# Cross-attention and spectral FFN on one core: the context's normalising moved ahead of the zero test, its low half ahead of the slot's other additions

## The chip, the cores and the metric

One NeuronCore of a Trainium2 chip runs the whole kernel. The metric is the device time of one execution in microseconds (us); the median of three runs stands for a kernel. The engines are TensorE (PE), VectorE (DVE), ScalarE (ACT), GpSimd (POOL) and SyncE (SP); each works through its own queue in program order, and they wait for one another by semaphores.

## What is computed

Two batches of 2048 rows of width 512 pass through a cross-attention of 16 heads over 128 keys, and then through a layer that multiplies in the frequency domain. Cut to what matters:

```python
def reference(x, ctx, mask, wq, bq, wk, bk, wv, bv, wo, bo, w_freq_real, w_freq_imag, bias):
    q = layernorm(x) @ wq + bq
    k, v = ctx @ wk + bk, ctx @ wv + bv
    score = q @ k.T / sqrt(32) * mask             # per head
    score = where(score == 0, -1e9, score)
    context = softmax(score) @ v                  # per head
    x = x + context @ wo + bo
    y = real(ifft(fft(layernorm(x)) @ (w_freq_real + 1j * w_freq_imag)))
    return x + y + bias
```

The output has the shape of x, (2, 2048, 512), in float32.

## The kernel before

The 4096 rows are cut into 16 chunks (c) of 256 rows (CH). The 16 heads are four groups (g) of four heads. A step s = 4c + g is the attention of one group of heads in one chunk; there are 64 (NS). Slots v run from 2 to 79, and in each slot every engine does its part of several steps at different ages, so that the steps overlap. The order inside a slot is written out by hand in each engine's block, and so is each wait. With r the remainder of v by 4, the parts of slot v around the change are:

- **TensorE** (items of `plan`, line 37, run at lines 609 to 619): it transposes the exponentials of step v-2 (`turn`, L582, two halves), runs the fill "WO" (output projection, r = 0 or 1) or "FF" (the frequency layer as one combined matrix, r = 2 or 3), both twelve products at L438, then the scores of step v+1 (`scores`, L570), then `weigh` of step v-3, which transposes the spread reciprocals (L595) and multiplies the exponentials by the values (L599), and at last the fill "Q", a later chunk's queries (L525, twelve products). Matrices go through TensorE as a high half and a low half in float16: each pair takes three products, high by high, high by low, low by high. Up to slot 11 the middle fills are instead "V", "U" and "M", which make the values and the combined matrix.
- **ScalarE** (L747 on): it copies the transposed reciprocals of step v-4 out of PSUM (`copy_rec`, L701), makes the exponentials of step v-1 (`exps`, L688; each with a read of the accumulator) in two halves with the copy of the transposed exponentials (`copy_pt`, L697) between them, then rounds the normalised context of step v-4 to float16 (`ctx_hi`, L708), then the high halves of the fills (`hi`, L662 for queries, L667 for the combined matrix) and of x1, the rows behind the attention (`norm_hi2`, L680).
- **VectorE** (L985 on): `mask_mul` (L860) multiplies the scores of step v by the mask out of PSUM; `zero_to_neg` (L867) turns zeros into the value that the softmax drops; `ctx_norm` (L883) multiplies the context of step v-4, in PSUM, by the copied reciprocals, into the tile cn; `least` (L872) takes the minimum of each head. Then the low halves and residuals of the fills (`lo`: L833 for queries, L839 for WO, L845 for FF; `low_m`, L851), statistics of rows (L897, L940) and the reciprocals of the sums (`recip`, L877).
- **GpSimd** (L1173 on): in some slots first the powers for a standard deviation (`rstd2`, L1060 and L1063, r = 1 or 2; `stat_cols`, L1030 to L1040, r = 0). From slot 9 on it waits for the slot's zero test (L1187), then adds the output bias to x in some slots (`add_bo`, L1053). `bias` (L1093) turns the minimum of step v into the bias of the exponentials. Then come the low half of x1 (`norm_lo2`, L1068, r = 2 or 3) or the addition of the layer's bias (`add_bf`, L1079, r = 0 or 1), then `ctx_lo` (L1104), the low half of the context of step v-4 into the tile cl, then the rest of the bias additions, `spread` (L1099), which copies the reciprocals of step v-2 for TensorE, and in r = 0 the scaling of a mask (L1086).
- **SyncE** loads and stores, and turns x1's halves with transposing DMAs (`turn_x1n`, L356) that wait for both halves.

Who waits for the two moved steps: `weigh` of step s waits for the context product of step s-1 (L590), since both use the bank CX; `ctx_hi` waits for it (L705) and `ctx_lo` for `ctx_hi` (L1103). The fill WO of a chunk waits for the chunk's four low halves (L535). `ctx_norm` of step s waits for `copy_rec` of step s (L880) and for `ctx_lo` of step s-2 (L882), because cn has two buffers.

```python
            def weigh(s):
...
                if s >= 1:
                    pe.wait_ge(cn_done, s)
...
                elif kind == "WO":
                    pe.wait_ge(o_lo, 2)
                    pe.wait_ge(ch_done, 4 * c + 4)
                    pe.wait_ge(p_cl, 4 * c + 4)
```

Of the kernel before, what the change touches and what calls it, by code (L numbers as in the profile page):

```python
# [18 lines left out]
NS = 4 * NC  # L19
# [70 lines left out]
def stats_slot(c, t):  # L90
    return 3 + t if c == 4 else 4 * (c - 4) + 2 + t


def small_slot(c):
    return 2 if c == 3 else 4 * (c - 3)
# [6 lines left out]
def lo_slot(c):  # L102
    return 3 if c == 3 else 6


def bo_slot(c):

    return c + 7 if c < 3 else 4 * c + 3 if c < 13 else 2 * c + 27


def build(nc, x, xt, ctx_in, mask, wq, bq, wk, bk, wv, bv, wo, bo, lparts, tables, bf, eye, sums, pick, places, heads, out):
# [3 lines left out]
    with ExitStack() as stack:  # L115
# [666 lines left out]
        def _(dve):  # L782
# [66 lines left out]
            def low_m(c):  # L849
                dve.wait_ge(m_hi, c + 1)  # L850
                dve.scalar_tensor_tensor(out=ml[:, c, :], in0=mf[:], scalar=SO / D, in1=mh[:, c, :],  # L851
                                         op0=ALU.mult, op1=ALU.subtract).then_inc(m_lo, 1)

            def mask_mul(s):
                c = s // 4
                dve.wait_ge(sc_done, 2 * s + 2)
                dve.wait_ge(p_ms, c + 1)
                if s >= NZ:
                    dve.wait_ge(pt_done, 2 * (s - NZ) + 2)
                dve.tensor_tensor(zs[:, s % NZ], A[:].rearrange("p t (h k) -> p t h k", h=4),  # L860
                                  ms[:, c % NM].unsqueeze(2).broadcast_to([128, 2, 4, KEYS]),
                                  ALU.mult).then_inc(tt_done, 1)

            def zero_to_neg(s):
                z = zs[:, s % NZ].rearrange("p t h k -> p (t h k)")
                dve.wait_ge(tt_done, s + 1)
                dve.scalar_tensor_tensor(out=z, in0=z, scalar=0.0, in1=z, op0=ALU.is_equal,  # L867
                                         op1=ALU.subtract).then_inc(eq_done, 1)

            def least(s):  # L870
                dve.wait_ge(eq_done, s + 1)
                dve.tensor_reduce(nmin[:, s % 4, :], zs[:, s % NZ].rearrange("p t h k -> p (t h) k"),  # L872
                                  AX.X, ALU.min).then_inc(mn_done, 1)

            def recip(s):
                dve.wait_ge(ex_done, s + 1)
                dve.reciprocal(rz[:, s % 4, :], zsum[:, s % 4, :]).then_inc(rz_done, 1)  # L877

            def ctx_norm(s):
                dve.wait_ge(rc_done, s + 1)  # L880
                if s >= 2:
                    dve.wait_ge(p_cl, s - 1)  # L882
                dve.tensor_tensor(cn[:, s % 2, :], CX[:, 0:256], rec[:, s % 2, :], ALU.mult).then_inc(cn_done, 1)  # L883
# [20 lines left out]
            def fold(n):  # L904

                q, i = divmod(n, 3)
                o1, o2 = ((ALU.add, ALU.add), (ALU.subtract, ALU.add),
                          (ALU.add, ALU.subtract), (ALU.subtract, ALU.subtract))[q]
                a, b, o = ((0, 1, o1), (2, 3, o1), (0, 2, o2))[i]
                if i == 0:  # L910
                    dve.wait_ge(d_lp[q], 16)
                if i == 2:
                    dve.wait_ge(l_hi, n - 6)
                a, b = 4 * q + a, 4 * q + b
                dve.tensor_tensor(lp[:, a, :], lp[:, a, :], lp[:, b, :], o).then_inc(l_hi, 1)

            def last_lo2(t):
                n = tile_of(NC - 1, t)
                dve.wait_ge(h2_done, n + 1)
                dve.tensor_tensor(x1nl[:, t], x1[:, n % NO, :], x1nh[:, t], ALU.subtract).then_inc(l2_done, 1)  # L920
# [64 lines left out]
            for v in range(V0, V1):  # L985
                c, r = divmod(v, 4)
                held, mids = slots[v][1:]
                if 0 <= v < NS:
                    mask_mul(v)
                if 0 <= v < NS:  # L990
                    zero_to_neg(v)
                if 0 <= v - 4 < NS:
                    ctx_norm(v - 4)
                if 0 <= v < NS:
                    least(v)
                if 0 <= v - 9 < 4:
                    low_m(v - 9)
                for n in held + mids:
                    lo(n)
                tasks = []  # L1000
                tasks += [(stats1, mean1, a, t) for a in range(4, NC) for t in range(2) if stats_slot(a, t) == v]
                if r == 0 and 0 <= c - 2 < NC:
                    tasks.append((stats2, mean2, c - 2, 0))
                if r == 1 and 0 <= c - 2 < NC:
                    tasks.append((stats2, mean2, c - 2, 1))
                for stats, _, *ct in tasks:
                    stats(*ct)
                if 0 <= v - 2 < NS:
                    recip(v - 2)
                for _, mean, *ct in tasks:  # L1010
                    mean(*ct)
                if c - 2 == NC - 1 and r < 2:
                    last_lo2(r)
                if v in (4, 5):
                    for n in range(3 * v - 6, 3 * v - 3):
                        fold(n)

        @block.gpsimd
        def _(pool):
# [69 lines left out]
            def bias(s):  # L1089
                pool.wait_ge(mn_done, s + 1)  # L1090
                if s >= 4:
                    pool.wait_ge(ex_done, s - 3)
                pool.tensor_scalar(nbias[:, s % 4, :], nmin[:, s % 4, :], NEG, None, ALU.mult).then_inc(p_nb, 1)  # L1093
# [7 lines left out]
            def ctx_lo(s):  # L1101
                c, g = divmod(s, 4)
                pool.wait_ge(ch_done, s + 1)  # L1103
                pool.tensor_tensor(cl[:, c % 2, g, :], cn[:, s % 2, :], ch[:, c % 2, g, :],  # L1104
                                   ALU.subtract).then_inc(p_cl, 1)
# [19 lines left out]
            def constant_row():  # L1125

                pool.wait_ge(g_done, at["U", 3] + 1)
                pool.memset(tb[0:1, 0, :], 0.5).then_inc(dc_done, 1)
# [44 lines left out]
            for v in range(V0, V1):  # L1173
                c, r = divmod(v, 4)
                if v == 8:
                    constant_row()
                if v <= VP and 0 <= v - 3 < NS:
                    spread(v - 3)
                for a in range(5, NC):
                    if small_slot(a) == v:  # L1180
                        stat_cols(a)
                if r == 1 and 0 <= c - 2 < NC:
                    rstd2(c - 2, 0)
                if r == 2 and 0 <= c - 2 < NC:
                    rstd2(c - 2, 1)
                if VS <= v < NS:
                    pool.wait_ge(eq_done, v + 1)  # L1187
                for a in range(5, NC):
                    if v == 4 * a - 11:
                        split_lo(a, slice(0, 2), False)  # L1190
                    if v == 4 * a - 10:
                        split_lo(a, slice(2, 4))
                for a in range(3, NC):
                    if bo_slot(a) == v:
                        add_bo(a, 0)
                    if bo_slot(a) + 1 == v and a >= 12:
                        add_bo(a, 1)
                if 0 <= v < NS:
                    bias(v)
                if r == 2 and 0 <= c - 2 < NC - 1:  # L1200
                    norm_lo2(c - 2, 0)
                if r == 3 and 0 <= c - 2 < NC - 1:
                    norm_lo2(c - 2, 1)
                if r < 2 and 0 <= c - 3 < NC:
                    add_bf(c - 3, r)
                if v == 3:
                    low_o()
                if 0 <= v - 4 < NS:
                    ctx_lo(v - 4)
                for a in (3, 4):  # L1210
                    if small_slot(a) == v:
                        stat_cols(a)
                for a in range(3):
                    if bo_slot(a) == v:
                        add_bo(a, 0)
                        add_bo(a, 1)
                for a in range(3, 12):
                    if bo_slot(a) == v:
                        add_bo(a, 1, slice(0, D // 2), False)
                    if bo_slot(a) + 3 == v:  # L1220
                        add_bo(a, 1, slice(D // 2, D))
                for a in (3, 4):
                    if lo_slot(a) == v:
                        split_lo(a)
                if v >= VP and 0 <= v - 2 < NS:
                    spread(v - 2)
                if r == 0 and 2 <= c + 1 < NC:
                    scale_mask(c + 1)
# [98 lines left out]
```

## Time and profile before

| | us |
|---|---|
| runs before | 460.48, 460.57, 462.78 |
| median | 460.57 |
| the profiled execution | 462.53 |
| its span | 460.7 |
| granted clock, mean over the span | 0.996 of full speed |

| engine | busy in the span, us |
|---|---|
| TensorE, matmuls | 443.5 |
| VectorE | 399.7 |
| ScalarE | 373.1 |
| GpSimd | 362.7 |

The profile is of one execution. The span runs from the first to the last instruction; the time has some 1.8 us more around it. Busy time is the sum of what an engine executed; waiting for a semaphore isn't counted. In a time line a row gives start and duration, the engine, the line, the operation, output and inputs, how many instructions were merged, and in brackets the idle time ahead of it with the engine and line that ended it. In a list of waits a row gives who waited for whom, the sum in us, how many times, and the longest.

### The profile page before, as it was taken

What the parts mean: (1) busy time and instruction counts of PE and PEld (TensorE: products, weight loads), DVE (VectorE), ACT (ScalarE), POOL (GpSimd) and SP (SyncE); (2) the same over time, 40 slices, a digit from 0 to 9 for tenths busy, and PEclk for the clock granted to TensorE, in tenths of its full rate; (3) what the DMA queues carried; (4) which work ended last, traced back from release to release, by engine and by line L of the source; (5) the groups of instructions that cost most, each with busy time, mean ns of one, the idle gap of its engine ahead of it and who ended that gap; (6) DMA issues with size and microseconds to landing.
All of it is one profiled execution on the core that took longest, in us unless ns stands there. A gap on an engine that the chain in (4) does not pass through costs nothing.

```text
span 460.7 us, 11172 instructions
## 1 busy us (share of the span) xinstructions
PE 443.5 (96%) x3510; PEld 293.2 (64%) x3510; DVE 399.7 (87%) x630; ACT 373.1 (81%) x1434; POOL 362.7 (79%) x540
## 2 busy tenths in 40 slices
PE   7989898998999999999999999999999999999997
PEld 5777676675666666666666666666666666555444
DVE  3797599899999999999999999999999898999443
ACT  3358587889898989899989898999989888999620
POOL 6588754795889899797989897979899686976663
PEclk9999999998999999999999999999999999999999
DMA  8997653322435454545545545355433334331244
GB/s 286 393 366 183 231 190 72 106 74 72 95 83 140 125 142 117 140 121 133 125 133 110 144 108 149 84 144 125 120 90 73 92 74 98 70 93 23 70 106 123
DMA packets 85287, 60.16 MB, mean 131 GB/s; under 512 B 40141, under 2 KB 72813, under 8 KB 84718
## 3 DMA queue, kind: packets, MB, share of 16 engines
q1 hardware_dynamic: 84508, 59.29, 47.4%
q8 instruction: 29, 0.48, 0.4%
q14 instruction: 28, 0.23, 0.2%
q10 hardware_dynamic: 722, 0.17, 0.2%
HBM read 29.33 MB, written 8.39 MB: 82 GB/s over the span
## 4 chain that ended last, share of the span: by engine, by line
PE 77%; DVE 10%; issue 4%; DMA 3%; SPq 2%; ACT 2%; POOL 1%; DVEq 0%; POOLq 0%; ACTq 0%
PE bank L438 33%; PE bank L525 17%; PE bank L582 10%; PE bank L599 7%; PE scores L570 5%; DVE zs L860 3%; PE bank L595 3%; PE bank L443 2%; SPq L276 2%; DMA cxs<-in_ctx 2%; DMA xs<-in_x 1%; DVE zs L867 1%; DVE nmin L872 1%; DVE st L897 1%; PE scores L443 1%
## 5 line engine op out<-in xcount | busy, mean ns | idle before, releaser
L688 ACT ACTIVATE zs<-zs,nbias 128x128 f32<-128x128 f32 x512 | 199.6, 397 | 5.2 <-POOL nbias L1093 5.2
L688 ACT ACTIVATION_READ_ACCUMULATOR zs<-zs,nbias 128x1 f32 x512 | 99.5, 194 | 0.0
L867 DVE SCALAR_TENSOR_TENSOR zs<-zs 128x1024 f32<-128x1024 f32 x64 | 80.7, 1262 | 2.3
L860 DVE TENSOR_TENSOR zs<-scores,ms 128x1024 f32<-128x1024 f32 x64 | 78.0, 1218 | 0.3 <-issue 0.3
L872 DVE TENSOR_REDUCE nmin<-zs 128x8 f32<-128x1024 f32 x64 | 77.4, 1209 | 0.1
L525 PE MATMUL bank<-xth,wqh 128*128 128x256 f16 x256 | 70.9, 277 | 2.9 <-DVE kl L810 2.0
L697 ACT COPY pt<-bank 128x512 f32<-128x512 f32 x128 | 68.5, 587 | 5.7 <-PE bank L582 5.2
L525 PE MATMUL bank<-xth,wql 128*128 128x256 f16 x256 | 70.2, 274 | 0.0
L525 PE MATMUL bank<-xtl,wqh 128*128 128x256 f16 x256 | 70.2, 274 | 0.0
L582 PE MATMUL bank<-ident,zs 128*128 128x128 f32 x512 | 67.0, 274 | 0.5 <-ACT zs L688 0.4
L1053 POOL TENSOR_TENSOR xs<-xs,bob 128x512 f32<-128x512 f32 (+1 forms) x41 | 42.3, 1035 | 24.6 <-DVE zs L867 24.6
L582 PEld LDWEIGHTS bank<-ident,zs 128*128 128x128 f32 x512 | 56.9, 141 | 5.2 <-ACT zs L688 3.5
L438 PE MATMUL bank<-woh,ch 128*128 128x512 f16 x128 | 48.5, 379 | 1.4 <-POOL cl L1104 1.4
L701 ACT COPY rec<-bank 128x256 f32<-128x256 f32 x64 | 23.9, 373 | 31.6 <-PE bank L599 31.4
L438 PE MATMUL bank<-woh,cl 128*128 128x512 f16 x128 | 48.5, 379 | 0.0
L438 PE MATMUL bank<-wol,ch 128*128 128x512 f16 x128 | 48.5, 379 | 0.0
L1104 POOL TENSOR_TENSOR cl<-cn,ch 128x256 f16<-128x256 f32 x64 | 44.9, 701 | 1.6 <-ACT ch L708 1.6
L438 PE MATMUL bank<-mh,x1h 128*128 128x512 f16 x120 | 45.5, 379 | 0.0
L438 PE MATMUL bank<-ml,x1h 128*128 128x512 f16 x120 | 45.5, 379 | 0.0
L438 PE MATMUL bank<-mh,x1l 128*128 128x512 f16 x120 | 45.5, 379 | 0.0
L833 DVE TENSOR_TENSOR ql<-bank,qh 128x256 f16<-128x256 f32 x64 | 26.7, 422 | 21.4 <-ACT qh L662 20.6
L525 PEld LDWEIGHTS bank<-xth,wqh 128*128 128x128 f16 x256 | 25.1, 98 | 27.7 <-issue 16.5
(118 smaller groups left out, 965.3 us busy)
## 6 DMA issues: line engine op xcount, KB each, us to landing
xs<-in_x SPq DMA_DIRECT2D x16, 512.0 KB, 4.1
xtr<-in_xt SPq DMA_DIRECT2D x16, 512.0 KB, 4.5
out<-x SPq DMA_DIRECT2D x31, 256.0 KB, 2.5
qs<-qh SPq DMA_DIRECT2D x120, 64.0 KB
lp<-in_lparts SPq DMA_DIRECT2D x4, 1024.0 KB, 9.7
qs<-ql SPq DMA_DIRECT2D x60, 64.0 KB
ms<-in_mask SPq DMA_DIRECT2D x16, 128.0 KB, 2.3
wqs<-in_wq SPq DMA_DIRECT2D x2, 512.0 KB, 6.5
```

The lines of the kernel that those rows point to most:

```text
L438: last = pe.matmul(o, a, b, start=(i == 0), stop=(i == len(mm) - 1))
L525: last = pe.matmul(o[:, 0:256], a, b, start=(i == 0), stop=(c > 1 and i == 11))
L582: last = pe.transpose(PB[f][:, a:a + 128], zs[:, s % NZ, t, 2 * f + i, :], ident[:])
L599: last = pe.matmul(CX[32 * j:32 * j + 32, 0:256], vs[:, b, h:h + 32], pt[:, s % 2, j, :], start=True, stop=True)
L688: last = act.activation(z, z, ACT.Exp, bias=nbias[:, s % 4, i:i + 1], scale=-NEG, accum_out=zsum[:, s % 4, i:i + 1])
L697: act.copy(pt[:, s % 2, 2 * f:2 * f + 2, :], PB[f][:]).then_inc(pt_copied, 1)
L833: last = dve.tensor_tensor(ql[:, c % 2, f, :], src[:, 0:256], qh[:, c % 2, f, :], ALU.subtract)
L860: dve.tensor_tensor(zs[:, s % NZ], A[:].rearrange("p t (h k) -> p t h k", h=4), ms[:, c % NM].unsqueeze(2).broadcast_to([128, 2, 4, KEYS]) ...
L867: dve.scalar_tensor_tensor(out=z, in0=z, scalar=0.0, in1=z, op0=ALU.is_equal, op1=ALU.subtract).then_inc(eq_done, 1)
L872: dve.tensor_reduce(nmin[:, s % 4, :], zs[:, s % NZ].rearrange("p t h k -> p (t h) k"), AX.X, ALU.min).then_inc(mn_done, 1)
L1053: i = pool.tensor_tensor(z, z, bob[:, n], ALU.add)
L1104: pool.tensor_tensor(cl[:, c % 2, g, :], cn[:, s % 2, :], ch[:, c % 2, g, :], ALU.subtract).then_inc(p_cl, 1)
```

## The change

On VectorE `ctx_norm` of slot v goes from behind `zero_to_neg` to ahead of it. On GpSimd `ctx_lo` goes from behind `norm_lo2`, `add_bf` and `low_o` to the place right behind `bias`. No operation is added or taken out, and no wait is changed.

```diff
@@ VectorE, loop over the slots
                 held, mids = slots[v][1:]
                 if 0 <= v < NS:
                     mask_mul(v)
+                if 0 <= v - 4 < NS:
+                    ctx_norm(v - 4)
                 if 0 <= v < NS:
                     zero_to_neg(v)
-                if 0 <= v - 4 < NS:
-                    ctx_norm(v - 4)
                 if 0 <= v < NS:
                     least(v)
@@ GpSimd, loop over the slots
                 if 0 <= v < NS:
                     bias(v)
+                if 0 <= v - 4 < NS:
+                    ctx_lo(v - 4)
                 if r == 2 and 0 <= c - 2 < NC - 1:
                     norm_lo2(c - 2, 0)
...
                     add_bf(c - 3, r)
                 if v == 3:
                     low_o()
-                if 0 <= v - 4 < NS:
-                    ctx_lo(v - 4)
```

## Rows read from the trace of the kernel before

**Rows 1.** The page: the span, and busy time (share) and instructions by engine.
```profile
span 460.7 us, 11172 instructions
PE 443.5 (96%) x3510; PEld 293.2 (64%) x3510; DVE 399.7 (87%) x630; ACT 373.1 (81%) x1434; POOL 362.7 (79%) x540
```

**Rows 2.** The chain that ended last, in time: start, us, what (225 to 245 us).
```profile
231.74 1.42 PE bank L525 x12
...
237.86 1.42 PE bank L525 x12
```

**Rows 3.** The list of waits, whole span: total us, times, longest.
```profile
ACT ch L708 <- DVE cn L883: 4.5, 6, 0.9
PE bank L438 <- POOL cl L1104: 1.4, 2, 0.8
PE bank L595 <- DVE cn L883: 1.2, 2, 0.9
```

**Rows 4.** The list of waits, 130 to 385 us.
```profile
ACT rec L701 <- PE bank L599: 23.8, 40, 1.1
DVE ql L833 <- ACT qh L662: 15.0, 31, 1.1
```

**Rows 5.** The time line of VectorE in a middle slot (start, us).
```profile
239.92 1.23 DVE L867 SCALAR_TENSOR_TENSOR zs<-zs 128x1024 f32<-128x1024 f32 x1
241.06 0.42 DVE L883 TENSOR_TENSOR cn<-bank,rec 128x256 f32<-128x256 f32 x1
```

**Rows 6.** The time line of GpSimd in the same slot.
```profile
240.13 1.60 POOL L1033 TENSOR_TENSOR rs<-ve,half 128x2 f32<-128x2 f32 x1
```

**Rows 7.** The time line of ScalarE in the same slot.
```profile
237.93 0.37 ACT L701 COPY rec<-bank 128x256 f32<-128x256 f32 x1 [1.13 <-PE bank L599]
```

**Rows 8.** The time line of TensorE in the head, its idle times from 108 us on.
```profile
110.21 0.62 PE L570 MATMUL scores<-ks,qs 102*128 102x128 f16 x8 [0.64 <-DVE zs L860]
111.85 0.50 PE L595 MATMUL bank<-ident,rzb 128*128 128x128 f32 x2 [1.02 <-issue]
...
126.08 0.41 PE L595 MATMUL bank<-ident,rzb 128*128 128x128 f32 x2 [0.23 <-issue]
```

**Rows 9.** Busy time by stretch: length, PE, PEld, DVE, ACT, POOL, granted clock, DMA.
```profile
112.00:115.70 3.70, 3.70 (x23) 1.99 (x23) 3.70 (x9) 3.17 (x13) 2.67 (x5) 0.54 0.18 55
```

**Rows 10.** The time line of VectorE in the head, 105 to 124 us.
```profile
105.48 1.71 DVE L851 SCALAR_TENSOR_TENSOR ml<-mf,mh 128x512 f16<-128x512 f32 x1 [0.56 <-ACT mh L667]
...
108.93 1.23 DVE L860 TENSOR_TENSOR zs<-scores,ms 128x1024 f32<-128x1024 f32 x1
...
111.33 0.42 DVE L883 TENSOR_TENSOR cn<-bank,rec 128x256 f32<-128x256 f32 x1
...
112.79 0.68 DVE L851 SCALAR_TENSOR_TENSOR ml<-mf,mh 128x512 f16<-128x512 f32 x1
...
119.75 1.60 DVE L851 SCALAR_TENSOR_TENSOR ml<-mf,mh 128x512 f16<-128x512 f32 x1 [0.60 <-ACT mh L667]
...
123.16 1.23 DVE L860 TENSOR_TENSOR zs<-scores,ms 128x1024 f32<-128x1024 f32 x1
```

**Rows 11.** The time line of GpSimd in the head.
```profile
105.48 1.16 POOL L1068 TENSOR_TENSOR x1nl<-x,x1nh 128x512 f16<-128x512 f32 x1
```

**Rows 12.** The time line of TensorE in the tail, the two waits for cl.
```profile
407.64 0.38 PE L438 MATMUL bank<-woh,ch 128*128 128x512 f16 x1 [0.62 <-POOL cl L1104]
...
428.32 0.38 PE L438 MATMUL bank<-woh,ch 128*128 128x512 f16 x1 [0.79 <-POOL cl L1104]
```

**Rows 13.** The time line of GpSimd in the tail.
```profile
397.90 1.40 POOL L1099 COPY rzb<-rz 128x256 f32<-128x256 f32 x1
...
426.19 0.23 POOL L1093 TENSOR_SCALAR nbias<-nmin 128x8 f32<-128x8 f32 x1 [1.36 <-issue]
...
427.51 0.67 POOL L1104 TENSOR_TENSOR cl<-cn,ch 128x256 f16<-128x256 f32 x1
```

**Rows 14.** The time line of ScalarE in the tail.
```profile
426.26 0.41 ACT L708 CAST ch<-cn 128x256 f16<-128x256 f32 x1
```

## The prediction, made before the changed kernel ran

> **What bounds the kernel now.** I read the page first: TensorE is busy 443.5 of a 460.7 us span, so only 17 us of it are idle [rows 1]. Then the chain of waits, in order of time. Between 112 and 385 us it is TensorE's own work without a break: the group of twelve query products starts at 231.74 and again at 237.86, one slot of 6.12 us [rows 2], and nearly the same spacing repeats over 40 times. In that stretch VectorE sat idle for ScalarE 15.0 us before the query residual and ScalarE 23.8 us for TensorE [rows 4]; both have slack, 0.3 to 1.1 us in most slots. What the change touches can therefore only pay where TensorE waits. The list of waits names those places: TensorE waited 1.2 us for the normalised context (cn) and 1.4 us for its low half (cl), ScalarE 4.5 us for cn [rows 3]. The time lines put them in the head, before 127 us, and in the tail, up to 428 us [rows 8, 12].
>
> **The change, part 1: the context product moves ahead of the zero test.** Nothing is added or removed: 64 products of 0.42 us and 64 zero tests of 1.23 us change places [rows 5]. The product starts 1.14 us after the operation ahead of it (241.06 against 239.92) and occupies 0.34 to 0.42 us. So cn is ready 1.14 us earlier, the zero test ends about 0.34 us later, and the minimum behind both starts when it did, give or take 0.1. No DMA is moved, and SyncE has no new step ahead of it. What is queued behind the zero test: GpSimd's gate (from slot 9 on it waits for the test before it adds the output bias) opens 0.34 us later. That is hidden: the next result, the bias for the exponentials, waits for the minimum anyway, and ScalarE has the 0.3 to 1.1 us above.
>
> In the middle stretch I cost all this at nothing: TensorE's own queue covers it, and if that cover went, each slot would pay up to 0.34 us.
>
> **In the head** it is worth more. TensorE waited 0.64 us for the masked scores of slot 11 and 1.02 us at 111.85 [rows 8]. The view calls the second "issue", but VectorE's product ran 111.33 to 111.75 [rows 10], 0.10 us before TensorE went on, so I take it for cn. Moved, the product starts at 108.93 + 1.14 = 110.07 and ends at 110.49, before the score matmuls are through (111.85 - 1.02 = 110.83). This wait goes: 1.0 us.
>
> Behind these two waits the granted clock averaged 0.54 over 3.70 us, that is mostly the lower level, 1.2 GHz [rows 9]. At full clock the same work takes 3.70 x 0.54 = 2.0 us, so the dip costs 1.7. Without the second wait TensorE idles 0.64 us there, or less, and I expect no dip. Lower bound of this term 0, upper 1.7. The Trainium skill, "TensorE: Matmul & The Clock Gate", section on the HAM clock gate, says the same in other words (idle TensorE is gated to half its rate); by it alone the dip could fall elsewhere, and the term would be 0.
>
> Part 2 has a share here: at 105.48 VectorE's residual of the combined matrix took 1.71 us, against 0.68 at 112.79 [rows 10], while GpSimd ran the low half of x1 (1.16 us) from 105.48 on [rows 11]. With the context's low half (about 0.68) first, the collision is some 0.5 us shorter. I take 0.5, bounds 0 and 1.0.
>
> These sum to 3.2 us, but VectorE is next late. At 119.75 it waited 0.60 us for ScalarE [rows 10], whose chain hangs on TensorE and moves up with it. So its masking product of slot 13 (123.16, 1.23 long) comes 0.5 + 0.6 = 1.1 us sooner and ends at 123.29; the scores follow 0.05 later and last 0.45; the context step at 126.08 [rows 8] then starts at 123.8, 2.3 us sooner. The smaller bound holds: 2.3. For new collisions with GpSimd I take 0.2 off: **head 2.1 us**, bounds 0.8 and 3.0. If the clock dips all the same, TensorE brings 1.0 + 0.5 and the 0.23 us wait at 126.08: 1.7.
>
> **Part 2: GpSimd makes cl ahead of the other additions.** 64 operations of about 0.67 us go ahead of one addition of about 1.2 us [rows 11], where the slot has one. In the middle they are needed a slot later: nothing. The transposes on SyncE's queue that take x1's low half start 0.67 us later; they are used four slots on, nothing.
>
> **In the tail** TensorE waits 0.62 and 0.79 us for cl, at 407.64 and 428.32 [rows 12], both times the output projection's first matmul. The second: GpSimd finished the bias at 426.19 + 0.23 = 426.42, then did x1's low half, and cl ran 427.51 to 428.18 [rows 13]. Its input was ready at 426.26 + 0.41 = 426.67 [rows 14]. First in the queue, cl would end at 426.67 + 0.67 = 427.34, sooner than TensorE is free (428.32 - 0.79 = 427.53): 0.8 us. The first wait gives at most 0.62, and part of it moves ScalarE's chain up, so the two add: up to 1.4.
>
> Against that: in the tail VectorE's and GpSimd's queues have almost no idle time, and they collide. At 397.90 a copy to spread the reciprocals (0.40 without hindrance) took 1.40 us because a zero test was running [rows 13]. With cl first, GpSimd must wait for ScalarE's half where it now works, some 0.4 us at the first slot of the tail, and the later zero test meets other operations. I take 0.5 off: **tail 0.9 us**, bounds -0.4 and 1.4. Waits at the other additions of the tail are covered by TensorE's groups of twelve products between them.
>
> **Sum.** 2.1 + 0.9 = 3.0 us. The profiled execution took 462.53 us (span 460.7 and 1.8 around it) and would take 459.5; it lies 1.96 above the median of 460.57, which becomes **457.6 us**. The runs may differ by just that clock dip; then the head gives 1.7 in them rather than 2.1, which is inside the range.
>
> **The rivals.** About 0.5% (2.3 us) is what a measurement of this kernel can tell from no change.
>
> 1. *Half of it.* One of the two places pays, or the clock dips again while VectorE's queue holds TensorE: 1.7 in the head and nothing in the tail gives 458.9, with a little lost 459.5. For: everything in the tail hangs on which of two engines starts first. Against: both waits are in the view with their releasers. Chance 0.27.
>
> 2. *Hidden anyway.* TensorE arrives earlier and waits for the masked scores instead, or the minimum decides all: 460.4. For: VectorE's queue is nearly full in the head, and its sum of work doesn't change. Against: the waits at 111.85 and 126.08 are for cn itself, ahead of the minimum. Chance 0.08.
>
> 3. *Slower: the zero test waits for GpSimd.* Now it starts 0.03 us behind the mask, often before GpSimd's next large operation: at 239.92 it ran 1.23 us, and GpSimd's power at 240.13 took 1.60 [rows 5, 6], some 0.9 more than it needs. Moved to 240.26 it would find that operation running and wait for it, 0.6 us. The Trainium skill, "SBUF — State Buffer", section "SBUF: two separate sides", has this as a rule: a VectorE operation with two SBUF inputs and a GpSimd one exclude each other, and whoever starts first holds the port throughout. The trace agrees so far (1.60 and 1.40 us for short operations). By it the power would no longer be held up and VectorE would. It decides once VectorE loses more than its slack, 15.0 us over 42 slots or 1.4 us in four [rows 4]. With one such collision in each of four slots, 2.4 us, 1.0 us of it comes through, in 11 groups of four 11 us; with one more in some, 2 to 5 us net of the gain: about 463. Against: only two slots of four have GpSimd's power there. Chance 0.10.
>
> 4. *The product waits itself.* If the reciprocal's copy were late, VectorE would stall ahead of the zero test. ScalarE made it at 237.93 to 238.30 [rows 7], the early product would start at 239.80: 1.5 us to spare. Were it late in the head, 0.5 us would be lost: 460. Chance 0.02.
>
> **How the numbers follow.** Forecast 0.53, with its own range of 456.3 to 458.4; rivals 0.27, 0.08, 0.10, 0.02. The range takes in the bounds of head and tail together (0.8 - 0.4 = 0.4 us at the least, 3.0 + 1.4 = 4.4 at the most; half a microsecond more below for waits of the early slots, which the list has too): 455.7 to 460.3; rival 3 and half of rival 2 are left out. Faster by over 0.5%: the forecast and a small part of rival 1, 0.60. Same: 0.30. Slower: 0.10.
>
> **What would show it.** Right: no wait of TensorE between the score matmuls and the context step near 110 us; granted clock 1.0 there; cl first behind each bias; no wait for cl in the tail; the same 6.12 us between. Wrong: zero tests of 1.5 us or more in the middle with slots above 6.12; a wait for masked scores at 110 to 125 us as long as the one removed; GpSimd's bias late in the tail, with ScalarE waiting for it.

## The result, and the profile after

| | before | after |
|---|---|---|
| median (range) of 6 runs each, us | 460.94 (460.44 to 462.78) | 458.61 (458.50 to 459.00) |
| ratio after / before, 95% interval | | 0.9947 [0.9935, 0.996] |
| profiled execution, us (its span) | 462.53 (460.7) | 458.93 (457.1) |
| mean granted clock in it | 0.996 | 0.996 |

The changed kernel is 0.53% faster by the ratio, 2.4 us (2.3 between the two medians); the forecast was 3.0 and 457.6 us. The profiled pair differs by more, 3.6 us, because the profiled execution of the kernel before was one of its slowest.

Where it came from is read by one mark: the start of the last query residual on VectorE (line 833), ahead of which lie head and middle. It was at 384.39 us of 460.7 before and is at 381.36 of 457.1 after. So the head and middle gave 3.03 us and the tail, 76.31 against 75.74, 0.57. Between the context step of slot 13 (126.08 before, 123.07 after) and the mark lie 258.31 and 258.29 us: the 3.0 us are all in the head.

The page after, against [rows 1]: less idle time of TensorE, and no new busy time of VectorE or GpSimd.

```profile
span 457.1 us, 11172 instructions
PE 442.1 (97%) x3510; PEld 293.3 (64%) x3510; DVE 398.0 (87%) x630; ACT 372.6 (82%) x1434; POOL 359.6 (79%) x540
```

The list of waits of the whole span, against [rows 3] (engine, line, what it waited for: total us, times, longest):

```profile
ACT zs L688 <- POOL nbias L1093: 7.9, 8, 3.3
POOL cl L1104 <- ACT ch L708: 5.8, 7, 2.5
PE bank L525 <- DVE ql L833: 2.0, 2, 1.6
ACT ch L708 <- DVE cn L883: 1.3, 2, 0.8
PE bank L595 <- POOL rzb L1099: 1.3, 2, 0.8
PE bank L438 <- POOL cl L1104: 0.8, 2, 0.6
```

TensorE's wait for cn is gone. Its waits for cl fell from 1.4 to 0.8 us, and they are not the same ones: the two of the tail went from 0.62 and 0.79 to nothing and 0.21, and one of 0.55 has come up in the head (at 113.91, below). In the early slots the wait for cn of 0.93 us became part of a wait for the query residual (ql), which has grown from 0.44 to 1.60 us. And a new one stands in the tail: 1.3 us for the copy that spreads the reciprocals (rzb).

The middle costs nothing. First the waits between 130 and 385 us, then busy time by stretch (length, PE, PEld, DVE, ACT, POOL, granted clock, DMA share, GB/s):

```profile
ACT rec L701 <- PE bank L599: 22.4, 38, 1.1
DVE ql L833 <- ACT qh L662: 14.3, 28, 1.1
ACT zs L688 <- POOL nbias L1093: 1.4, 3, 0.8
```

```profile
66.00:74.00 8.00, 6.40 (x43) 4.66 (x42) 7.93 (x13) 5.87 (x23) 4.68 (x10) 0.79 0.29 88
112.00:115.70 3.70, 3.15 (x22) 1.96 (x20) 3.66 (x9) 3.64 (x15) 3.15 (x6) 1.00 0.51 167
126.00:384.00 258.00, 258.00 (x2114) 168.14 (x2113) 240.57 (x376) 233.84 (x929) 222.76 (x338) 1.00 0.46 117
```

TensorE is busy in 258.00 of 258.00 us (257.92 before), and the slack of the others is about as before [rows 4]. ScalarE's 1.4 us for the bias (nbias) there delay nothing on TensorE. At 112 us the granted clock is 1.00 where it was 0.54 [rows 9]. But a dip has come up at 66 to 74 us, with 0.79.

TensorE in the head (start, us, engine line, operation, idle time before and who ended it), against [rows 8]:

```profile
70.39 0.39 PE L525 MATMUL bank<-xth,wqh 128*128 128x256 f16 x1 [1.60 <-DVE ql L833]
...
109.65 0.62 PE L570 MATMUL scores<-ks,qs 102*128 102x128 f16 x8
110.11 0.39 PE L595 MATMUL bank<-ident,rzb 128*128 128x128 f32 x2
...
113.91 0.38 PE L438 MATMUL bank<-woh,ch 128*128 128x512 f16 x1 [0.55 <-POOL cl L1104]
...
123.07 0.39 PE L595 MATMUL bank<-ident,rzb 128*128 128x128 f32 x2
```

The context step follows its score matmuls without the 1.02 us. TensorE then stands 0.55 us for cl at the output projection of slot 12, where it did not stand in the trace before. The context step of slot 13 starts at 123.07 where it was 126.08. VectorE in the same stretch, against [rows 10]:

```profile
105.89 0.73 DVE L851 SCALAR_TENSOR_TENSOR ml<-mf,mh 128x512 f16<-128x512 f32 x1 [0.84 <-ACT mh L667]
108.37 1.23 DVE L860 TENSOR_TENSOR zs<-scores,ms 128x1024 f32<-128x1024 f32 x1
109.51 0.42 DVE L883 TENSOR_TENSOR cn<-bank,rec 128x256 f32<-128x256 f32 x1
118.64 0.68 DVE L851 SCALAR_TENSOR_TENSOR ml<-mf,mh 128x512 f16<-128x512 f32 x1
121.12 1.23 DVE L860 TENSOR_TENSOR zs<-scores,ms 128x1024 f32<-128x1024 f32 x1
```

Both residuals ml that took 1.71 and 1.60 us now take 0.73 and 0.68. On GpSimd, cl stands where x1's low half stood at 105.48 [rows 11]:

```profile
105.41 0.67 POOL L1104 TENSOR_TENSOR cl<-cn,ch 128x256 f16<-128x256 f32 x1
106.04 1.61 POOL L1068 TENSOR_TENSOR x1nl<-x,x1nh 128x512 f16<-128x512 f32 x1
```

In the tail, TensorE, against [rows 12]; then VectorE, GpSimd and ScalarE of the slots in which its new waits stand:

```profile
396.99 0.41 PE L595 MATMUL bank<-ident,rzb 128*128 128x128 f32 x2 [0.82 <-POOL rzb L1099]
402.46 0.41 PE L595 MATMUL bank<-ident,rzb 128*128 128x128 f32 x2 [0.43 <-POOL rzb L1099]
423.41 1.09 PE L582 MATMUL bank<-ident,zs 128*128 128x128 f32 x8 [0.67 <-ACT zs L688]
424.72 0.38 PE L438 MATMUL bank<-woh,ch 128*128 128x512 f16 x1 [0.21 <-POOL cl L1104]
```

```profile
387.25 0.67 POOL L1104 TENSOR_TENSOR cl<-cn,ch 128x256 f16<-128x256 f32 x1 [0.57 <-ACT ch L708]
393.68 0.40 ACT L688 ACTIVATE zs<-zs,nbias 128x128 f32<-128x128 f32 x1 [0.86 <-POOL nbias L1093]
394.77 1.82 DVE L867 SCALAR_TENSOR_TENSOR zs<-zs 128x1024 f32<-128x1024 f32 x1
395.44 1.40 POOL L1099 COPY rzb<-rz 128x256 f32<-128x256 f32 x1
399.95 2.11 DVE L867 SCALAR_TENSOR_TENSOR zs<-zs 128x1024 f32<-128x1024 f32 x1
```

The zero tests of these two slots took 1.38 and 1.50 us before. GpSimd stands 0.57 us at 387.25 for ScalarE's half of the context, six microseconds later its bias is late, and ScalarE waits 0.86 us for it. That the wait goes on from there to TensorE is tested below (`e9_slot56_old`).

### The profile page after: what moved, and what is told of

Its sections match the earlier page's. It is cut to its first block, busy times and chain, and to the rows that moved or that the text cites. A ratio compares the mean times of both kernels' runs of the same rounds, so it can differ in the third digit from the quotient of the medians.

```text
span 457.1 us, 11172 instructions
## 1 busy us (share of the span) xinstructions
PE 442.1 (97%) x3510; PEld 293.3 (64%) x3510; DVE 398.0 (87%) x630; ACT 372.6 (82%) x1434; POOL 359.6 (79%) x540
## 4 chain that ended last, share of the span: by engine, by line
PE 79%; DVE 10%; issue 5%; ACT 3%; DMA 1%; ACTq 0%; POOL 0%; DVEq 0%
PE bank L438 32%; PE bank L525 17%; PE bank L582 10%; PE bank L599 6%; PE scores L570 5%; PE bank L443 4%; DVE zs L867 3%; PE bank L595 3%; DVE zs L860 1%; ACT zs L688 1%; DMA bqb<-in_bq 1%; PE scores L443 1%; DVE cn L883 1%; ACT pt L697 1%; DVE x L845 1%
## 5 line engine op out<-in xcount | busy, mean ns | idle before, releaser
L1104 POOL TENSOR_TENSOR cl<-cn,ch 128x256 f16<-128x256 f32 x64 | 43.3, 677 | 6.0 <-ACT ch L708 5.8
```

## The experiments

The theory: two waits of one chain were removed, and each needs the other; what lies over the forecast in the profiled pair comes from collisions between VectorE and GpSimd, what lies under it in the tail too. The rivals: one of the two moves does it all; the clock does it; the moved product itself makes the tail's collisions. All kernels of one comparison share the runs of the kernel before.

**One move alone.** `e1_vector_only` has the first hunk of the diff alone, `e2_gpsimd_only` the second.

> Only the VectorE half of the change. Theory A (the context product ahead of the zero test frees TensorE near 110 us, and GpSimd's half adds to it): the wait of 1.02 us there goes, but the output projection of slot 12 then waits over 1 us for cl instead of 0.55, and the waits for cl in the tail come back: 0.8 to 1.7 us faster than before. Rival B (GpSimd's half brings it, by the shorter collision at 105 us and the waits for cl): 0 to 0.5 us faster.

> Only the GpSimd half. Theory A: the wait for cn in the head stays (about 1 us near 110 us), the residual of the combined matrix at 105 us is 0.5 to 1.0 us shorter, the cl waits of the tail shrink: 0.6 to 1.4 us faster than before. Rival B: nearly all of the change's 2.4 us.

Measured: 460.19 us (12 runs, 0.9978 [0.9963, 0.9993]) and 460.22 (12 runs, 0.9973 [0.996, 0.9987]). TensorE's time line in the head, first of `e1_vector_only`, then of `e2_gpsimd_only`:

```profile
109.68 0.39 PE L595 MATMUL bank<-ident,rzb 128*128 128x128 f32 x2
114.60 0.38 PE L438 MATMUL bank<-woh,ch 128*128 128x512 f16 x1 [1.68 <-POOL cl L1104]
```

```profile
111.33 0.41 PE L595 MATMUL bank<-ident,rzb 128*128 128x128 f32 x2 [1.02 <-issue]
114.43 0.38 PE L438 MATMUL bank<-woh,ch 128*128 128x512 f16 x1
```

With the product alone, TensorE gets at once past the context step and then stands 1.68 us for cl at the output projection. With cl alone that wait is absent and the 1.02 us before the context step is back. Either way the projection starts at 114.4 to 114.6; with both it starts at 113.47 in the next kernel.

Against the median of the kernel before, 461.33 in this comparison, each move alone gives 1.1 us, and above both gave 2.4. But that median isn't the kernel's lowest level. Of its 30 runs 18 lie at 461.2 and above, and of the 24 runs with one move only one does. Later experiments ask what makes these upper levels. Against the 12 runs below them (median 460.57) each move alone gives 0.3 to 0.4 us.

The traces agree. The context step of slot 13 starts at 123.76 with the product moved alone and at 123.99 with cl alone; with the old head at its best (`e4_both_tail` below) it is 123.98, with both moves 122.63. In the tail, behind the mark, lie 76.33 us with the product alone and 75.99 with cl alone, against 76.31 and 75.74 for none and both. So head and tail together, the moves are worth about 0.2 and 0.3 us alone and 1.9 together: each needs the other. The rest of each 1.1 us is that the upper levels are rare or gone.

Two of the 12 runs of `e1_vector_only` (460.86 and 461.45) have a mean clock of 0.996, though the 1.02 us wait is gone from its trace; where the clock dipped in them no trace shows.

**Head and tail apart.** `e3_both_head` makes both moves for slots below 16 only, `e4_both_tail` from slot 54 on; the other slots keep the old order.

```diff
-                if 0 <= v - 4 < NS:
+                if 0 <= v - 4 < NS and (v < 16):
                     ctx_norm(v - 4)
...
-                if 0 <= v - 4 < NS:
+                if 0 <= v - 4 < NS and (v < 16):
                     ctx_lo(v - 4)
```

> Both halves in slots 2 to 15 only, the old order from slot 16 on. Theory A: the head gives 1.7 to 2.4 us and the tail is as before. Rival (the tail gives most of what the medians show, and the 3 us of the profiled head are a dip of the granted clock that most runs don't have): under 1 us.

> Both halves from slot 54 on only. Theory A: 0.3 to 0.9 us faster than before, with the 1.02 us wait near 110 us unchanged; zero tests of 1.8 and 2.1 us in the tail as in the changed kernel. Rival: 1.5 us or more.

Measured: 459.11 (7 runs, 0.9949 [0.9931, 0.9967]), 2.3 us faster, and 460.62 (12 runs, 0.9991 [0.9974, 1.0008]); this ratio can't show the tail's part. Four of these 12 runs, at 462.2 to 462.5, have a mean clock of 0.996: the head is the old one. The zero tests of the tail took 1.82 and 2.13 us, as expected. The mark shows the tail's part: behind it lie 76.36 us in `e3_both_head` and 75.81 in `e4_both_tail`. Over all profiles of this study the kernels with the old tail have 76.31 to 76.41 (4 of them), those with the changed one 75.74 to 75.82 (5). So the tail gives 0.6 us.

The head of `e4_both_tail` is the old one, and yet it isn't that of the profile before. Its two engines at 105 us:

```profile
105.68 0.69 DVE L851 SCALAR_TENSOR_TENSOR ml<-mf,mh 128x512 f16<-128x512 f32 x1 [0.55 <-ACT mh L667]
105.70 1.70 POOL L1070 TENSOR_TENSOR x1nl<-x,x1nh 128x512 f16<-128x512 f32 x1
```

VectorE started 0.02 us ahead of GpSimd and took 0.69 us; the one that lost was GpSimd, 1.70 instead of 1.16. Before, the two starts read 105.48 both [rows 10, 11] and VectorE took 1.71. The kernel before thus has more than one time. Its 30 runs of this comparison lie at 460.4 to 461.0 (12), at 461.2 to 461.5 (11), at 462.0 (2) and at 462.7 to 463.3 (5, all with a mean clock of 0.996). The next two kernels ask what makes the levels.

**The clock.** `e6_before_filled_11` is the kernel before with eight idle matmuls where TensorE otherwise stands for cn; their bank is overwritten later.

```diff
                 else:
                     weigh(item[1])
+                if item == ("S", 12, 1):
+                    pe.wait_ge(pt_copied, 19)
+                    for i in range(8):
+                        pe.matmul(PB[0][:, 0:256], wqh[:, 0, 0:128], wqh[:, 0, 0:256], start=True, stop=True)
```

> The kernel before, with eight idle products of 256 columns (about 0.9 us) put into TensorE's wait for cn in slot 11; they write a bank that is overwritten, the output is the same. Theory A (the dip of the granted clock at 112 us costs the kernel before about 1.5 to 2 us in those runs that have it, and comes of the 1.0 us wait): no run with a mean clock of 0.996 and none above 462; the median is 0 to 0.5 us below the kernel before, whose fast level (460.4) stays: the wait itself is still there. Rival (the dip has another cause): runs of 462.4 and more remain, one in five.

Measured: 460.60 (12 runs, 460.38 to 461.81; 0.9991 [0.9977, 1.0006]). No run had a mean clock below 0.999; of the kernel before, 3 of 19 had on this chip, at 462.9 to 463.1. TensorE's time line and the stretch at 112 us of this kernel:

```profile
110.94 1.04 PE L623 MATMUL bank<-wqh 128*128 128x256 f16 x8
112.12 0.41 PE L595 MATMUL bank<-ident,rzb 128*128 128x128 f32 x2
...
115.74 0.38 PE L438 MATMUL bank<-woh,ch 128*128 128x512 f16 x1 [0.35 <-POOL cl L1108]
```

```profile
112.00:115.70 3.70, 3.27 (x30) 2.35 (x30) 3.70 (x10) 3.58 (x14) 2.40 (x4) 1.00 0.25 84
```

Its profiled execution took 461.37 us, and the two engines near 105 us were:

```profile
105.75 1.71 DVE L855 SCALAR_TENSOR_TENSOR ml<-mf,mh 128x512 f16<-128x512 f32 x1 [0.56 <-ACT mh L671]
105.76 1.16 POOL L1072 TENSOR_TENSOR x1nl<-x,x1nh 128x512 f16<-128x512 f32 x1
```

VectorE lost the race here, and there was no dip. So the level of 461.4 is the lost race, and the one near 462.8 is the lost race with a clock dip on top, 1.4 to 1.5 us. Part of that price is a collision: without the dip the next residual, at 119.34, took 0.68 us, while with it, at 119.75, it took 1.60 [rows 10]. In three runs of twelve the filled kernel is still at 461.4 to 461.8.

That the filling prevents the dip is likely, not shown. The wait isn't enough for a dip: it stood at 0.98 to 1.02 us in `e2_gpsimd_only` and `e10_before_slot10` (next), without the whole 0.64 us ahead of it, and none of their 23 runs dipped. With the old head, all runs with a mean clock of 0.996 have the time of a lost race and a dip, so only lost races count, and the filled kernel has three of them. On this chip three of the kernel before's six runs above 461.1 dipped.

**The race.** `e10_before_slot10` is the kernel before with cl ahead in slot 10 alone.

```diff
+                if 0 <= v - 4 < NS and (v == 10):
+                    ctx_lo(v - 4)
```

> The kernel before, with GpSimd's low half of the context moved ahead in slot 10 alone. Theory (the residual of the combined matrix at 105.5 us and GpSimd's low half of x1 start within 0.1 us of each other, and the order in which they fall makes the kernel before's levels of 460.5, 461.4 and, with the dip of the clock, 462.8 us): the two upper levels go, nearly all runs lie from 460.2 to 461.0. Rival (the levels come from elsewhere): runs at 461.4 and 462.8 as often as before.

Measured: 460.72 (11 runs, 460.45 to 460.97; 0.9997 [0.9988, 1.0006]). None lies above 461.0, where the kernel before has 5 of 15. Both engines of it at 105 us:

```profile
105.70 0.69 DVE L851 SCALAR_TENSOR_TENSOR ml<-mf,mh 128x512 f16<-128x512 f32 x1 [0.55 <-ACT mh L667]
105.72 1.20 POOL L1104 TENSOR_TENSOR cl<-cn,ch 128x256 f16<-128x256 f32 x1
```

One GpSimd operation in another order takes the upper levels away and leaves the median alone (0.1 us). It doesn't speed up the kernel, it steadies it. No run of the kernel before dipped on this chip either (none of 15), though four or five of them lost the race; whether that is chance isn't settled.

**The changed kernel again, and its first slots.** `e5_changed_again` repeats the change on another chip. `e8_from_slot6` leaves the product in its old place for slots 4 and 5, so that the two waits joined to 1.60 us at 70.39 come apart again.

```diff
-                if 0 <= v - 4 < NS:
+                if 0 <= v - 4 < NS and (v >= 6):
                     ctx_norm(v - 4)
```

> The changed kernel itself, as the mark for the others on this chip: 458.6 us, two levels 0.4 us apart at most by the dip of the granted clock near 71 us; no run above 459.2, where the kernel before has runs from 460.4 to 463.3.

> The changed kernel, with the context product behind the zero test in slots 4 and 5 as before. Theory (moving cn in slot 5 only joins two waits of TensorE, 0.93 and 0.44 us, into one of 1.60 us, because the query residual decides): 458.2 to 458.6 us, and no dip of the clock at 71 us. Rival (cn early in slot 5 is worth its 0.9 us): 0.5 us or more slower than the changed kernel.

Measured: 458.54 (6 runs, 0.9943 [0.9924, 0.9963]) and 458.32 (6 runs, 0.994 [0.9921, 0.996]). The rival is out: without the early product in slots 4 and 5 the kernel is no slower. TensorE of `e8_from_slot6`:

```profile
68.79 0.41 PE L595 MATMUL bank<-ident,rzb 128*128 128x128 f32 x2 [0.97 <-DVE cn L883]
70.20 0.28 PE L525 MATMUL bank<-xth,wqh 128*128 128x256 f16 x1 [0.43 <-DVE ql L833]
```

The 0.2 us between the medians needn't be the edit's. TensorE's first matmul that waits for a load (L477) starts at 8.78 us in the trace of `e5_changed_again` and at 8.44 in this one, and from there to the mark both take 372.30 us.

Neither had a dip, so the pair can't say whether splitting the wait prevents one. In the first runs of the changed kernel it fell in two of six (458.93 and 459.00, the others at most 458.64) and cost 0.4 us. Over the study the mean clock was 0.996 in 3 of 27 runs of the kernels with both moves and the joined wait, and in none of the 21 of the four kernels with the product moved from slot 6 on; that is too few to tell.

**The tail.** `e7_spread_first_tail` is the change with the reciprocals' copy right behind cl from slot 57 on. `e9_slot56_old` is `e8_from_slot6` with GpSimd's old order in slot 56, where it stood 0.57 us. `e11_slots58_59_old` is `e8_from_slot6` with the product's old place in slots 58 and 59, where the zero tests are long. `e12_from_slot6_again` is the base of these last two on the same chip; `e7_spread_first_tail` has `e5_changed_again` (458.54, 75.82 behind the mark) for its base.

```diff
+                if v >= 57 and 0 <= v - 2 < NS:
+                    spread(v - 2)
...
-                if 0 <= v - 4 < NS:
+                if 0 <= v - 4 < NS and (v != 56):
                     ctx_lo(v - 4)
...
-                if 0 <= v - 4 < NS and (v >= 6):
+                if 0 <= v - 4 < NS and (v >= 6 and v not in (58, 59)):
                     ctx_norm(v - 4)
```

> The changed kernel with GpSimd's copy of the reciprocals right behind cl from slot 57 on, ahead of the larger addition. Theory (in the tail TensorE waits 0.82 and 0.43 us for this copy, which a zero test holds up for 1.0 us): those waits go, 0.3 to 1.0 us faster than the changed kernel. Rival (the exponentials' bias on GpSimd decides the tail): within 0.2 us.

> The changed kernel with the context product moved from slot 6 on only, and GpSimd's old order in slot 56, where with the new one it stands 0.57 us before cl for ScalarE's half. Theory (this wait is what makes GpSimd's bias late in the next slot, for which ScalarE waits 0.86 us): that wait falls to about 0.3 us and the tail is 0.3 to 0.6 us shorter. Rival (VectorE's zero tests in the tail decide): within 0.15 us of the same kernel with the new order in slot 56.

> The changed kernel with the product moved from slot 6 on, but not in slots 58 and 59, where the moved zero test took 1.82 and 2.11 us. Theory (the loss in the tail is the collision of zero test and GpSimd's addition): zero tests of 1.4 to 1.5 us there, but TensorE waits for cn again, 0.3 and 0.4 us, in place of the copy: 0 to 0.4 us faster. Rival: slower by 0.1 to 0.3.

> The mark for the other three: the changed kernel with the product moved from slot 6 on. 458.3 us, no dip of the granted clock in any run.

| kernel | median, us | ratio [interval] | behind the mark, us |
|---|---|---|---|
| `e7_spread_first_tail` | 459.08 (8) | 0.9956 [0.9941, 0.9971] | 76.35 |
| `e9_slot56_old` | 458.09 (5) | 0.9942 [0.993, 0.9955] | 75.31 |
| `e11_slots58_59_old` | 458.98 (5) | 0.9961 [0.9949, 0.9974] | 76.22 |
| `e12_from_slot6_again` | 458.78 (5) | 0.9953 [0.994, 0.9967] | 75.74 |

TensorE in the tail of `e7_spread_first_tail`, then of `e11_slots58_59_old`:

```profile
397.38 1.09 PE L582 MATMUL bank<-ident,zs 128*128 128x128 f32 x8 [0.93 <-ACT zs L688]
402.82 1.09 PE L582 MATMUL bank<-ident,zs 128*128 128x128 f32 x8 [0.51 <-ACT zs L688]
```

```profile
396.63 0.41 PE L595 MATMUL bank<-ident,rzb 128*128 128x128 f32 x2 [0.85 <-DVE cn L883]
402.12 0.41 PE L595 MATMUL bank<-ident,rzb 128*128 128x128 f32 x2 [0.45 <-DVE cn L883]
```

Both forecasts failed. `e7_spread_first_tail` is 0.5 us slower than its base where 0.3 to 1.0 faster was expected, and all that the tail had gained is lost. `e11_slots58_59_old` is 0.2 us slower, as its rival had it, with 0.48 more behind the mark. In both, the wait stays about as long or grows (0.82 and 0.43 in the changed kernel) and its name changes. The copy made early frees the context step, and TensorE then stands for the exponentials. The product in its old place doesn't shorten the zero tests, 2.03 and 2.13 us, and puts TensorE behind cn. So neither the copy nor the product's place in these two slots is the cause. ScalarE and TensorE in `e9_slot56_old`:

```profile
392.91 0.40 ACT L688 ACTIVATE zs<-zs,nbias 128x128 f32<-128x128 f32 x1 [0.37 <-POOL nbias L1095]
...
396.24 0.41 PE L595 MATMUL bank<-ident,rzb 128*128 128x128 f32 x2 [0.34 <-POOL rzb L1101]
401.73 0.41 PE L595 MATMUL bank<-ident,rzb 128*128 128x128 f32 x2 [0.45 <-POOL rzb L1101]
```

Here the first waits do shrink, ScalarE's from 0.86 to 0.37 and TensorE's from 0.82 to 0.34, while the second on TensorE stays (0.43 and 0.45). The first long zero test is back at 1.39 us and the second still takes 2.13. The tail is shorter by 0.43 us. So GpSimd's stand in slot 56 cost the tail 0.43 us. On this chip the kernel beats its base by 0.7 us, more than its tail explains. The rest is in the first loads. The base was forecast at 458.3 and measured at 458.78, with two levels (458.3 twice, 458.8 to 459.0 three times). Its trace, of the run at 459.04, has:

```profile
9.16 0.70 PE L477 MATMUL bank<-bqb,selb 128*128 128x256 f32 x2 [0.93 <-DMA bqb<-in_bq]
```

In `e9_slot56_old` this matmul starts at 8.85, and from it to the mark `e9_slot56_old` takes 372.24 us and the base 372.30. All seven traces of kernels with both moves in the head and no dip lie at 372.24 to 372.31, so such differences are the loads' and no edit's. `e9_slot56_old` is the best version of the study: 458.09 against 460.83, with no run above 458.20.

## Why the prediction was right, and where it was off

**The product ahead of the zero test, wait of 1.0 us.** Right: it went. What the prediction didn't weigh is that this wait and that for cl are one chain. With the product alone it turns to 1.68 us at the projection, and with both moves 0.55 us of it still stand there. "The smaller bound holds", VectorE next late, was right as well, and harder than forecast. In `e3_both_head` against the head of `e4_both_tail`, neither with a lost race or a dip, the masking product of slot 13 starts at 120.69 against 120.91, only 0.2 us sooner; the context step of that slot starts at 122.63 against 123.98, 1.35 us sooner. The other 1.1 us are the product's move in that slot, and the forecast's 2.3 us has that part at 1.2 (1.1 for the mask, the rest behind it). So this part of the mechanism was right in kind and size.

**The collision in the head: 0.5 us.** This is the term whose size failed. The collision at 105.48 was sized well: ml ended at 107.19 and ends at 106.62 in the changed kernel, 0.57 us, and the masking product behind it moves by as much (108.93 to 108.37). But [rows 10] has a second one, the ml of 1.60 us at 119.75, and I let its start move up without asking whether it would still collide. It doesn't: before, GpSimd's addition had started at 119.53, 0.22 ahead of it; now the residual starts at 118.64 and is 0.68 long, 0.92 less. With it the mask starts at 121.12, 2.04 us sooner where 1.1 was forecast, and the head gives 3.03 in the profiled pair instead of 2.1. This second collision came with the clock dip: in the trace of the lost race without a dip (`e6_before_filled_11`) the same residual took 0.68 us. The forecast gave the dip a price on TensorE and none through VectorE.

**The clock.** The dip at 112 us went, as forecast. Its price, taken at 1.7 us from TensorE alone, is 1.4 to 1.5 by the levels of the kernel before (461.4 and 462.8). The Trainium skill, "TensorE: Matmul & The Clock Gate", section on the HAM clock gate, has the clock follow how busy TensorE has been of late. The trace after agrees, with 0.79 at 66 to 74 us around a wait of 1.60 us; a second of the six runs has the same mean clock of 0.996. Its price is 0.4 us, probably because VectorE bounds that stretch (busy 7.93 of its 8.00 us).

**The tail: 0.9 us.** It gave 0.57 to 0.6. Both waits for cl shrank as forecast (0.62 to nothing, 0.79 to 0.21). The term of 0.5 for collisions was undersized: 1.4 less what the tail gave makes it 0.8. It named the cause, some 0.4 us of GpSimd waiting for ScalarE's half at the tail's first slot, and that was 0.57 in slot 56; without it the tail gives 1.0. In the forecast it was a lump sum instead of a chain to be followed: late bias, late exponentials, zero test meeting GpSimd (1.82 us), late copy, TensorE.

**From the profile to the median.** I took the same 3.0 us off both. The profiled execution held a lost race and a dip that the median didn't, and those were part of what the change removes. Level by level: 460.5, less 1.35 in the head and 0.6 in the tail, is 458.55, and the six runs without a dip in `e5_changed_again` have a median of 458.54. The forecast 457.6 was 1.0 too low from this and the tail. The sentence that other runs might give 1.7 in the head pointed there and should have carried the number. The 3.0 us came as near to the measured 2.3 as it did partly by luck: at the lowest level the change is worth 1.95, and the other 0.4 are in the median before, 460.94, which stands between two levels (three of its six runs at 460.4 to 460.6, three at 461.3 and above).

**Slips in the working.** The product's start against the mask was put 1.14 us earlier; by [rows 10] it is 2.40 less 1.14, so 1.26 (the time of 110.07 is worked out rightly). The least gain of 0.4 us gives 460.2, not 460.3, as the range's end. And rival 3's 463 doesn't follow from its 11 us, which less the gain give 468.6.

**The rivals.** *Half of it* was the nearest to the median. *Hidden anyway* is refuted by `e3_both_head`. *The zero test waits for GpSimd*: the Trainium skill, "SBUF — State Buffer", section "SBUF: two separate sides", has it that whoever starts first keeps the port. The traces agree where the starts lie 0.02 us apart or more: VectorE was ahead by 0.02 in `e4_both_tail` (0.69 and 1.70 us). Closer than that the profile's times don't tell the winner: in `e6_before_filled_11` VectorE reads 0.01 ahead and lost (1.71 and 1.16). In the middle it never decided. This is the zero test over all 64 slots (min, median, max in ns):

```profile
L867 DVE SCALAR_TENSOR_TENSOR zs<-zs x64: 1214/1217/2111, 23.7 to 420.8; 128x1024 f32<-128x1024 f32 x64
```

The median is 1.22 us, and the two longest (1.82 and 2.11 us) are in the tail. *The product waits itself*: its waits for the reciprocal's copy add up to 0.6 us in two places before and to 0.5 in one after, so the earlier place added none.

## What to carry to other kernels

When a short operation that another engine waits for is moved ahead of a long one, do it at every link of the chain: one link alone gave 0.3 to 0.4 us at the lowest level and moved the wait to the next, both gave 1.9. Compare level with level: the medians alone said 1.1 and 2.4, since the kernel before ran at an upper level in 18 of 30 executions. Look for starts of two engines within a few hundredths of a microsecond where the durations say that they exclude each other: who wins decides 0.9 us here, and a forecast made from an execution in which one lost must say what the others give. A mark inside the program, and a second behind the first loads, tell the edit's part from the rest within 0.1 us. An engine made to wait for an input earlier than it must passes that on, so exempt the slots in which the input is late.

## What the hardware showed that was not expected

- Some 0.02 us between the starts of VectorE's residual and GpSimd's low half decide whether VectorE takes 0.69 or 1.71 us, and show in the kernel's time as levels 0.9 us apart (460.5 and 461.4). VectorE won when it read 0.02 us ahead (`e4_both_tail`, `e10_before_slot10`) and lost when it read 0.01 ahead (`e6_before_filled_11`) or level [rows 10, 11]. The 1.71 us are the other's whole 1.16 and 0.55 of its own.
- The granted clock fell to the lower level behind 1.66 us of idle time in two pieces (0.64 and 1.02, [rows 8, 9]) in the trace before. Executions with the same mean clock (0.996) are 5 of 30 and 3 of 19 of that kernel, 4 of 12 of `e4_both_tail`, and none of 15 on a third chip. With the second piece filled by eight matmuls they are none of 12, and none of 12 where the first piece was 0.33 us (`e2_gpsimd_only`).
- With the changed head and no dip, TensorE waits near 82 us for a DMA (qs from srow): 0.38 us in `e3_both_head`, 0.30 in `e5_changed_again`, none in the kernel before. The four kernels with the product moved from slot 6 on wait 0.54 to 0.61 us there, and no kernel here removes it.

What stays open: why the first loads end up to 0.9 us apart (8.25 to 9.16 over all traces); the few runs at 462.0; where the two dips of `e1_vector_only` fell; whether the filling prevents the dip; and whether a joined wait of 1.60 us makes a dip likelier than two of 0.97 and 0.43.
